# Fp4 FFN: the gate's four group sums through one ScalarE copy and a chain of three VectorE adds, in place of two halves and a GpSimd add

## What is computed

```python
w_gu = _dequant_fp4(gate_up_packed, gate_up_scales, 128)   # values * scale of (row, group of 128 inputs)
w_down = _dequant_fp4(down_packed, down_scales, 128)
gate_up = einsum('bsh,oh->bso', x, w_gu)
gate, up = gate_up[..., :1408], gate_up[..., 1408:]
h = silu(gate) * up
y = einsum('bsi,hi->bsh', h, w_down)
y = y / sqrt(mean(y * y) + 1e-6);  x = layernorm(x + y)
```

## Time and profile before

| | |
|---|---|
| median of 3 runs | 1869.16 us (1864.07 to 1870.29) |
| the profiled execution | 1868.6 us, span 1866.8 us |
| busy share of the span | TensorE 86%, VectorE 70%, ScalarE 50%, GpSimd 36% |
| fp4 stage, from its first transposes | 1524 us to the end of the span |
| gate copies L2324 | 88, mean 688 ns |
| gate adds L2423 | 88, 750 ns median |
| GpSimd gate sums L2304 | 44, mean 1296 ns |

### The profile page before, as it was taken

How to read it: one execution, slowest core, us unless ns; L and a number is a source line. 1 busy time by engine, 2 the same in 40 slices (tenths; PEclk the granted TensorE clock), 3 DMA queues, 4 the chain that set the end, 5 groups by cost and what they waited for, 6 DMA issues and landing times. The chain is left out here.

```text
span 1866.8 us, 26478 instructions
## 1 busy us (share of the span) xinstructions
PE 1607.2 (86%) x8780; PEld 1134.2 (61%) x8812; DVE 1304.0 (70%) x2366; ACT 940.1 (50%) x1932; POOL 677.4 (36%) x634
## 2 busy tenths in 40 slices
PE   7999967999846899996699989999859969999996
PEld 5788744555524556564466666566527756677774
DVE  6476644666858899995467586684937969866674
ACT  3221215776655666654356466464615535655553
POOL 4034406676522232331222132322203315565564
PEclk9999988999978999998799999999979989999998
DMA  6200007533020000000512112121104210000000
GB/s 203 68 23 1 0 16 210 176 118 92 23 92 1 1 1 1 1 1 1 163 36 69 52 52 69 43 79 50 35 31 150 64 34 1 1 24 0 24 23 23
DMA packets 66850, 95.73 MB, mean 51 GB/s; under 512 B 12176, under 2 KB 28688, under 8 KB 66716
## 3 DMA queue, kind: packets, MB, share of 16 engines
q1 hardware_dynamic: 58460, 80.40, 14.0%
q0 software_dynamic: 6144, 12.60, 2.5%
q10 hardware_dynamic: 2112, 1.05, 0.2%
HBM read 56.25 MB, written 4.19 MB: 32 GB/s over the span
## 5 line engine op out<-in xcount | busy, mean ns | idle before, releaser
L2522 PE MATMUL bank<-fp_xT,fp_weights_values 128*128 128x512 f32 x704 | 185.5, 402 | 14.5 <-DVE fp_gate L2423 12.8
L1455 ACT ACTIVATE causal_probs<-bank,causal_neg 128x512 f32<-128x512 f32 (+3 forms) x256 | 134.4, 531 | 113.7 <-DVE causal_neg L1546 74.2
L2522 PEld LDWEIGHTS bank<-fp_xT,fp_weights_values 128*128 128x128 f32 x704 | 129.9, 190 | 58.0 <-DVE fp_gate L2423 19.9
L736 ACT ACTIVATE heads_probs<-bank,heads_neg 128x512 f32<-128x512 f32 x128 | 88.3, 690 | 102.5 <-DVE heads_neg L765 102.2
L765 DVE TENSOR_REDUCE heads_neg<-bank 128x1 f32<-128x512 f32 x128 | 87.2, 681 | 74.4 <-PE bank L810 74.2
L2547 PE MATMUL bank<-fp_wd,fp_hT 128*128 128x512 f32 x528 | 133.3, 393 | 4.7 <-DVE X L2445 3.5
L1349 POOL DMA_DIRECT2D causal_qS<-causal_qk x96 | 48.2, 509 | 227.7 <-DVE causal_qk L1504 227.7
L2432 DVE SCALAR_TENSOR_TENSOR fp_up<-bank,fp_weights_scales,fp_up 128x512 f32<-128x512 f32 x132 | 99.1, 751 | 44.4 <-ACT fp_up L2330 36.2
L910 POOL TENSOR_TENSOR ternary_z<-ternary_z 128x1024 f32<-128x1024 f32 x16 | 37.7, 2356 | 220.3 <-DVE ternary_z L1053 220.3
L2547 PEld LDWEIGHTS bank<-fp_wd,fp_hT 128*128 128x128 f32 x528 | 98.5, 188 | 28.5 <-issue 6.7
L1148 PE MATMUL bank<-weights_raw,ternary_qT 128*128 128x512 bf16 x433 | 104.6, 387 | 8.9 <-ACT weights_raw L606 5.4
(11 more groups left out here) (276 smaller groups left out, 4136.0 us busy)
## 6 DMA issues: line engine op xcount, KB each, us to landing
heads_xd<-X SPq DMA_DIRECT2D x64, 128.0 KB, 2.6
heads_cd<-in_ctx SPq DMA_DIRECT2D x64, 128.0 KB, 2.7
causal_qS<-causal_qk SPq DMA_DIRECT2D x96, 64.0 KB, 2.8
causal_qS<-causal_qk POOLq DMA_DIRECT2D x96, 64.0 KB, 2.5
causal_kS<-causal_qk SPq DMA_DIRECT2D x96, 64.0 KB, 2.6
causal_kS<-causal_qk POOLq DMA_DIRECT2D x96, 64.0 KB, 2.4
X<-in_x SPq DMA_DIRECT2D x4, 1024.0 KB, 7.7
heads_cT<-in_ctxT SPq DMA_DIRECT2D x4, 1024.0 KB, 5.6
```

The source lines that it names most:

```text
L736: act.activation(probs[:, n % 4], banks[n % 3][:], ACT.Exp, bias=neg[:, g % 2, k:k + 1], accum_out=total[:, g % 2, k:k + 1]).then_inc(prob ...
L1455: act.activation(probs_of(i)[:, h + one], view[:, one], ACT.Exp, bias=neg[:, G % 2, at:at + 1], accum_out=total[:, G % 2, at:at + 1]).then ...
L2522: last = pe.matmul(banks[4 + g][:], values[:, g, n % NI, of], xT[:, part, g], start=part == 0, stop=part == 1)
```

## The change

ScalarE now copies only bank 4 (`first_gate`). VectorE adds banks 5, 6 and 7 to the same tile in a chain, each waiting for the one before (`rest_of_gate`). The second gate tile and GpSimd's sum go; silu waits for the third VectorE add, and TensorE's `up` of group 2 now waits for a VectorE add instead of a ScalarE copy. All else is as it was.

```diff
 # gpsimd, per step
-                pool.wait_ge(gate_odd, 2 * n + 2)
-                pool.tensor_tensor(gate[:, n % 2, 0], gate[:, n % 2, 0], gate[:, n % 2, 1], ALU.add).then_inc(gate_summed, 1)
                 if n:
                     low(n - 1)
...
-                pool.tensor_tensor(up[:, n % 2], up[:, n % 2], gate[:, n % 2, 0], ALU.mult).then_inc(h_ready, 1)
+                pool.tensor_tensor(up[:, n % 2], up[:, n % 2], gate[:, n % 2], ALU.mult).then_inc(h_ready, 1)
 # scalar
-            def even(n, g):
+            def first_gate(n):
                 if n >= 2:
                     act.wait_ge(h_ready, n - 1)
-                act.wait_ge(gate_ready, NG * n + g + 1)
-                act.activation(gate[:, n % 2, g // 2], banks[4 + g][:], ACT.Copy, scale=scale(n, g, 0)).then_inc(gate_even, 1)
+                act.wait_ge(gate_ready, NG * n + 1)
+                act.activation(gate[:, n % 2], banks[4][:], ACT.Copy, scale=scale(n, 0, 0)).then_inc(gate_first, 1)
...
-                act.wait_ge(gate_summed, n + 1)
+                act.wait_ge(gate_rest, 3 * n + 3)
...
-                even(n, 0)
-                even(n, 2)
+                first_gate(n)
 # vector
-            def odd(n, g):
-                dve.wait_ge(gate_even, 2 * n + g // 2 + 1)
+            def rest_of_gate(n, g):
+                if g == 1:
+                    dve.wait_ge(gate_first, n + 1)
+                else:
+                    dve.wait_ge(gate_rest, 3 * n + g - 1)
                 dve.wait_ge(gate_ready, NG * n + g + 1)
...
-                odd(n, 1)
-                odd(n, 3)
+                for g in range(1, NG):
+                    rest_of_gate(n, g)
 # tensor, gate_up
-                        pe.wait_ge(*((gate_odd, 2 * n + g // 2 + 1) if g % 2 else (gate_even, 2 * n + g // 2 + 1)))
+                        pe.wait_ge(*((gate_rest, 3 * n + g) if g else (gate_first, n + 1)))
```

More of the change, by code:

```diff
@@ L2232, in fp4_ffn @@
         xT = m.sbuf("xT", [P, 2, NG, S], F32R)
-        gate = m.sbuf("gate", [P, 2, 2, S])
+        gate = m.sbuf("gate", [P, 2, S])
         up = m.sbuf("up", [P, 2, S])
@@ L2245, in fp4_ffn @@
         x_turned, x_high, x_low = (m.sem(n) for n in ("x_turned", "x_high", "x_low"))
-        gate_ready, gate_even, gate_odd, gate_summed, silu_ready = (
-            m.sem(n) for n in ("gate_ready", "gate_even", "gate_odd", "gate_summed", "silu_ready"))
+        gate_ready, gate_first, gate_rest, silu_ready = (
+            m.sem(n) for n in ("gate_ready", "gate_first", "gate_rest", "silu_ready"))
         up_ready, up_first, up_rest = (m.sem(n) for n in ("up_ready", "up_first", "up_rest"))
@@ L2332, in silu @@
             def silu(n):
-                act.wait_ge(gate_summed, n + 1)
-                act.activation(gate[:, n % 2, 0], gate[:, n % 2, 0], ACT.Silu).then_inc(silu_ready, 1)
+                act.wait_ge(gate_rest, 3 * n + 3)
+                act.activation(gate[:, n % 2], gate[:, n % 2], ACT.Silu).then_inc(silu_ready, 1)
             def high(n):
@@ L2417, in x_lows @@
                     dve.tensor_tensor(xT[:, 1, g], banks[4 + g][:], xT[:, 0, g].bitcast(F32), ALU.subtract).then_inc(x_low, 1)
-            def odd(n, g):
-                dve.wait_ge(gate_even, 2 * n + g // 2 + 1)
+            def rest_of_gate(n, g):
[3 more added lines that the diff above has]
+                    dve.wait_ge(gate_rest, 3 * n + g - 1)
                 dve.wait_ge(gate_ready, NG * n + g + 1)
-                part = gate[:, n % 2, g // 2]
-                dve.scalar_tensor_tensor(out=part, in0=banks[4 + g][:], scalar=scale(n, g, 0), in1=part, op0=ALU.mult,
-                                         op1=ALU.add).then_inc(gate_odd, 1)
+                dve.scalar_tensor_tensor(out=gate[:, n % 2], in0=banks[4 + g][:], scalar=scale(n, g, 0), in1=gate[:, n % 2],
+                                         op0=ALU.mult, op1=ALU.add).then_inc(gate_rest, 1)
             def rest(n, g):
```

## The result

The kernel after takes 1881.42 us (median of 7 runs, 1877.78 to 1884.07) against 1870.04 us before (7 runs, 1864.07 to 1871.41): a ratio of 1.0062, 95% interval 1.0051 to 1.0073. The forecast was 1883.6, range 1873.5 to 1888. The profiled execution took 1880.06 us, with a span of 1878.0.

What follows compares the result with a forecast made beforehand. The prediction took VectorE to bound batch 0 and TensorE the later batches. It summed 4.8 + 9.7 - 0.4 + 0.7 = +14.8 us on the profiled 1868.6, and forecast a median of 1883.6, range 1873.5 to 1888.

Steps and rivals of the forecast that it cites:

- The chain: Batch 0: three gate adds on VectorE, each waiting for the last, cost about +0.60 us a step, +4.8 in all.
- The hold: Batch 0: GpSimd's low, issued earlier, keeps VectorE's L2407 waiting, 1.66 instead of 0.69 us: +0.97 a step.
- Its count: Batch 0: low keeps VectorE waiting in each of steps 1 to 10, +9.7 us in all.
- the list of signs: What the profile after would show, such as L2407 at 1.66 us in ten of eleven cases and 8.9 us steps.
- part 2: GpSimd's sum goes and low moves up, delaying L2407, or L2400 in steps 8 to 10: +9.7 us.
- Step 11 and the batch ends: End of batch 0 and later batches: -0.4 us by estimate for step 11, +0.7 for the later batches.
- the +0.56: Later batches, behind i = 5: VectorE comes late from normalise, so the third gate add reaches TensorE 0.56 us late.
- The chain without the hold: Rival, 12%: L2407 in batch 0 is not kept waiting by GpSimd, leaving +5.1 us, 1874.
- The clock follows: Rival, 7%: TensorE's clock falls in batch 0, its matmuls bound the step, 1.4 us more in ten steps, 1897.
- No change: Rival, 7%: VectorE's idle in batch 0 takes up the third adds and low escapes the two-SBUF-input operations, 1870.
- Faster: Rival, 4%: late silu puts GpSimd's product behind L2394 in batch 0, -1.1 us in each of ten steps, 1863.

Runs made afterwards that it cites:

- e1: Kernel after, with GpSimd's low(n - 1) in steps 1 to 11 also waiting for the first gate add of step n: 1875.09 us, ratio 1.0027.
- e5: Kernel after, with ScalarE doing high(n - 1) ahead of first_gate(n) in steps 1 to 11: 1885.64 us, ratio 1.0082.
- e3: Kernel after, with GpSimd's product waiting for d_weigh(n) in batch 0 and ScalarE doing d_highs and first before high: 1864.01 us, ratio 0.9969.
- e2: Kernel before, with low(n - 1) ahead of the sum of the two gate tiles in GpSimd's queue: 1881.09 us, ratio 1.0057.

## Why the forecast was right, point by point

- **The chain, +4.8.** Right: 4.6 us by e1. The third add lengthens the gate's adds by 0.92, of which the idle and the overlap give 0.33 back, as the earlier trace rows let one work out. The 0.2 too much lies in step 1, for which the forecast had +0.12 and e1 has -0.06 (7.86 against 7.92 us), and in steps of 0.57 where it had 0.60. An ordinary step of e1 is 7.89 us, where 7.33 + 0.60 gives 7.93. The Trainium skill's "VectorE: DVE Perf Modes", section "The DRAIN you can't avoid", in whose test eight copies take as long with a semaphore after each as with one after the last, would by the prediction's estimate have made it 7.33 + 0.33 = 7.66; the trace does not agree.
- **The hold, +0.97 a step.** The mechanism and its size were right to the hundredth: L2404 ends at M + 2.63, with fp16 inputs too. That the operation issued first keeps the other out is what the Trainium skill says in "SBUF — State Buffer", section "Who interferes with whom", and both orders are in the profile after: 1.65 us for L2404 where low was waiting, 1.38 to 1.84 us for low where L2404 had begun. Where L2397 is held instead, the length is not quite the same: 1.48 against 0.43 us, 1.05, and e5's steps 8 and 9 take 9.25 us where e1's take 8.21.
- **Its count, ten.** This is the term that was mis-sized: five. "Now nothing holds it but high(n - 1)", with high "at M + 0.13 at the latest", was read from one step and left out what holds high: first_gate of the next step, ahead of it in ScalarE's queue, and so TensorE. Two of the five misses, steps 3 and 10, stood in the trace of the kernel before, where high starts at M + 1.51 and M + 5.32. The other three, steps 5, 7 and 9, come from the change: a hold makes VectorE late, that stalls TensorE, the clock falls behind the stall, and TensorE's late gate lets the next low miss. With that tie cut (e5) the count is ten, seven of L2406 and three of L2399 (the list of signs had L2407 in all ten; part 2 has it right), and batch 0 costs 14.4 us.
- **Step 11 and the batch ends.** x_lows to the first add -1.0 where I had -0.9. The waits for L2445 vanish altogether, 1.2 each, where I expected 0.7 to remain, but a good part of that is TensorE arriving later. The late gate adds behind `statistics` and `normalise` cost more than the +0.56: with the 0.46 gained at each batch end added back, the two batches from add to add are +1.2 and +0.8, so the sum of the later batches is +1.7, not +1.2.
- **The rivals.** "The chain without the hold" is e1, 1875.1, where the forecast had 1874. "The clock follows": the clock did fall, to 0.56, but in short stretches in which VectorE bound the step; TensorE's work stayed hidden but for 0.24 us in steps 6 and 8. So a clock under 1.00 between 1560 and 1620, which the prediction named as the sign of this rival, was there without it. "No change" is out, with the whole interval above 1.005. "Faster" had its mechanism right (the product behind L2394 frees 1.1 us a step: e3), but nothing in this change brings it about.

In sum, +14.8 was forecast and the spans differ by 11.2: five holds of 0.97 too many (-4.9), the chain 0.2 dearer in the forecast than in the chip, and in the other direction some 0.6 for the waits of the held steps behind free ones, 0.5 for the later batches, and small differences of both signs in the stretches forecast at nothing (+1.1, -0.4, -0.3). That the median came out within 2.2 us of the forecast is in part luck: the count was off by 4.9 us, and terms that nobody forecast gave some of it back. The range, which began at the chain alone, would have held with any count from none to ten.

## What to carry to other kernels

Removing an operation from an engine's queue moves up all that stands behind it: ask what the next operation will run beside, not only what it no longer waits for. In this kernel L2404 with its two SBUF inputs (1.65 us against 0.69) and the bit operation L2391 (1.38 against 0.29) want GpSimd idle beside them, while the gate's three adds, which read PSUM, take 2.32 us in e1 with low under them and 2.31 in e5 without. Moving one product there and ScalarE's order after it was worth more (1864.01 against 1881.42) than the change under study; the product alone gave 1876.12. When counting how often a collision happens, follow both parties' queues back, through every engine that stands ahead of them, in every step and not in one.

## What was not expected of the hardware

- The length of a stall of TensorE doesn't tell whether the clock falls. In the kernel after, 1.74 us of idle were followed by a granted clock of 0.73 and then 0.56 over 4.9 us, after which it was 1.00 again. In e2, 1.82 us were followed by 0.50, but 1.81, 1.63 and 1.86 us by 1.00, and so were 3.08 us in its step 2 and 2.06 us in the kernel before.
- TensorE running at half clock made the next step shorter (7.87 us from gate adds to gate adds, where the same step takes 8.85 in e5), because an operation of GpSimd then came too late to hold VectorE.
- A GpSimd subtraction that waits for a VectorE operation gets in ahead of the next VectorE operation, although that follows within 0.04 us: in all seven steps of e5 in which it waited for L2399 with L2406 next.
